# x of two batches brought into the output sum by a TensorE matmul and copied out by ScalarE, and one key-value product moved from GpSimd to VectorE, with all engine queues written in a new order

## What is computed

```
xn = (x - mean) / sqrt(var + eps)
qkv = xn @ w_qkv.T                      # 16 heads of 8
q, k = code products (2 codes per head)
q = softmax(q) * scale
k_exp = exp(k - max over rows of k)
kv = cumsum(k_exp * v) / cumsum(k_exp)  # over the rows of a batch
attn = (q . kv) @ w_out.T
gate, up = fp4(xn) @ fp4(w_gate).T, fp4(xn) @ fp4(w_up).T      # 352 columns
ffn = fp4(silu(gate) * up) @ fp4(w_down).T
out = x + attn + ffn
```

## Time and profile before

| | |
|---|---|
| median of three runs | 129.69 us (129.6 to 129.81) |
| profiled execution, its own time | 129.76 us |
| its span, from first to last instruction | 128.0 us |
| granted TensorE clock, mean | 1.000 |
| TensorE matmul busy | 123.7 us (97%) |
| TensorE weight load busy | 104.7 us (82%) |
| VectorE busy | 119.3 us (93%) |
| ScalarE busy | 103.4 us (81%) |
| GpSimd busy | 116.4 us (91%) |

### The profile page before, as it was taken

The page is one execution under the profiler, slowest core; times in us unless marked ns, Lnnn a source line. Parts: engine busy times, 40 slices in busy tenths (PEclk is TensorE's granted clock), DMA queues, the critical chain, the costliest instruction groups (busy, mean ns, idle before and its releaser), DMA issues.

```text
span 128.0 us, 2411 instructions
## 1 busy us (share of the span) xinstructions
PE 123.7 (97%) x805; PEld 104.7 (82%) x805; DVE 119.3 (93%) x275; ACT 103.4 (81%) x272; POOL 116.4 (91%) x130
## 2 busy tenths in 40 slices
PE   6999999999999999999999999999999999999992
PEld 6988777676666778987678989998877989999991
DVE  3888999999999999999999999999999999999951
ACT  1498989999999998999979489479979976827740
POOL 5499999999999999999999999999999999998800
PEclk9999999999999999999999999999999999999999
DMA  4994000000000000002000020020002000202031
GB/s 101 282 348 176 0 10 3 0 0 0 0 0 0 0 5 0 0 13 74 0 0 3 3 82 5 0 82 0 0 0 82 5 0 0 82 0 87 0 110 54
DMA packets 4363, 5.14 MB, mean 40 GB/s; under 512 B 576, under 2 KB 2432, under 8 KB 4352
## 3 DMA queue, kind: packets, MB, share of 16 engines
q1 hardware_dynamic: 3552, 4.69, 10.6%
q10 hardware_dynamic: 800, 0.31, 0.9%
HBM read 2.90 MB, written 2.10 MB: 39 GB/s over the span
## 4 chain that ended last, share of the span: by engine, by line
PE 79%; ACT 7%; POOL 6%; DVE 3%; DMA 2%; issue 1%; POOLq 0%
PE ps L1905 17%; PE ps L1888 13%; PE ps L1885 11%; PE ps L1892 8%; PE ps L1856 7%; PE ps L1897 5%; PE ps L1875 3%; PE ps L1870 3%; PE ps L1876 3%; DMA x_all<-x 2%; PE ps L1881 2%; PE ps L1865 2%; PE ps L1837 2%; PE ps L1851 2%; POOL yx L374 2%; POOL o_codes L394 2%
## 5 line engine op out<-in xcount | busy, mean ns | idle before, releaser
L1905 PE MATMUL ps<-w_t,hq_t 128*128 128x128 f32 x192 | 25.1, 275 | 0.0
L1905 PEld LDWEIGHTS ps<-w_t,hq_t 128*128 128x128 f32 x192 | 23.7, 192 | 1.6 <-DVE qh L1343 0.3
L399 POOL TENSOR_TENSOR yh<-h,h_r 128x704 f32<-128x704 f32 (+1 forms) x20 | 23.0, 1155 | 0.5 <-ACT h_r L713 0.3
L1888 PE MATMUL ps<-w_t,xq_t 128*128 128x352 f32 x64 | 22.6, 463 | 0.0
L1885 PE MATMUL ps<-w_t,xq_t 128*128 128x352 f32 x64 | 21.6, 463 | 0.0
L404 POOL TENSOR_TENSOR hq<-qh,h_max 128x704 f32<-128x704 bf16 (+1 forms) x16 | 19.9, 1245 | 0.1
L719 ACT ACTIVATE hq_t<-ps 128x384 f32<-128x384 f32 x32 | 15.0, 486 | 5.9 <-PE ps L1892 5.9
L390 POOL TENSOR_TENSOR kv<-kv 128x288 f32<-128x288 f32 x24 | 19.3, 804 | 0.3
L384 POOL TENSOR_TENSOR kv<-v_sb,kv 128x1024 f32<-128x1024 f32 x8 | 15.8, 1977 | 0.3 <-ACT kv L684 0.2
L394 POOL TENSOR_TENSOR o_codes<-kv,q_n 128x1024 f32<-128x1024 f32 (+1 forms) x9 | 16.0, 1779 | 0.0
L1885 PEld LDWEIGHTS ps<-w_t,xq_t 128*128 128x128 f32 x64 | 11.4, 190 | 5.3 <-DVE h L1299 0.5
(11 more groups left out here) (126 smaller groups left out, 297.4 us busy)
## 6 DMA issues: line engine op xcount, KB each, us to landing
x_all<-x SPq DMA_DIRECT2D x8, 256.0 KB, 4.9
out<-out_sb SPq DMA_DIRECT2D x7, 256.0 KB, 2.0
out<-out_sb SPq DMA_DIRECT2D x4, 64.0 KB, 1.6
w_raw<-w_down SPq DMA_DIRECT2D x1, 176.0 KB, 4.6
w_raw<-w_up ACTq DMA_DIRECT2D x1, 128.0 KB, 3.3
w_raw<-w_gate SPq DMA_DIRECT2D x1, 128.0 KB, 3.3
wqk_raw<-w_qkv ACTq DMA_DIRECT2D x1, 128.0 KB, 5.3
wqkv_t<-w_qkv SPq DMA_DIRECT2D x1, 64.0 KB, 4.8
```

The lines of the kernel that those rows point to most:

```text
L399: return nc.gpsimd.tensor_tensor(blocks(yh[:, p, lo * FF:hi * FF], n), h[:, p, lo * HB:hi * HB, 0:BLOCK], spread(h_r[:, p, lo * HB:hi * HB ...
L1888: return nc.tensor.matmul(ps[:, bank, 0:FF], xq_t[:, b % 2, j * P:(j + 1) * P], w_t[:, FFP:FFP + FF], start=True, stop=True)
L1905: last = nc.tensor.matmul(ps[:, bank, j * P:(j + 1) * P], hq_t[:, b % 2, j, c * P:(c + 1) * P], w_t[:, 2 * FFP + c * P:2 * FFP + (c + 1) * P],
```

## The change

Two edits change what is computed where.

1. For batches 0 and 1, `add_x` multiplies the identity with x (one matmul of 512 columns, f32) into the bank in which the output is summed, as the first matmul there. When `project` and `down` have been added, ScalarE's `keep_out` copies the bank to `out_sb`. VectorE's `residual` of these two batches is gone. SyncE's queue waits for `outk_done` instead of `resid_done` for their stores.
2. For batch 0, `k_times_v_from` on VectorE reads v straight from the bank that `qkv` wrote and multiplies it by exp(k), in two instructions of 512 elements. GpSimd's `k_times_v(0)` and ScalarE's `keep_v(0)` are gone.

With them, the queues of all engines are written in a new order. What is new in kind there: `x_dequant` of batch 2 moves from VectorE to GpSimd (and its `x_grid` writes SBUF instead of the bank); `warm_input()` moves on VectorE from ahead of `guards()` to behind `negative_mean(0, 1)`; eight `unread()` stand at the start instead of seven and fifteen in all instead of sixteen; `qk_weights` and its copy come ahead of the first transposes; batch 0's gates all stand behind `w_transpose('up')`, where two of them stood before it. The cut diff:

```diff
+            def keep_out(b, bank):
+                return nc.scalar.activation(out_sb[:, b % 2, :], ps[:, bank, :], ACT.Copy)
...
+            def k_times_v_from(b, bank):
+                p = b % 2
+                for a in range(2):
+                    last = nc.vector.tensor_tensor(kv[:, p, 2 * a:2 * a + 2, 0:KV].rearrange("p j (c h w) -> p j c h w", c=CODE, w=HEAD),
+                                                   halves(bank)[:, a, :, HEADS + HC:].rearrange("p j (h w) -> p j h w", w=HEAD).unsqueeze(2).broadcast_to([P, 2, CODE, HEADS, HEAD]),
+                                                   kv[:, p, 2 * a:2 * a + 2, KV:ROW].rearrange("p j (c h) -> p j c h", c=CODE).unsqueeze(4).broadcast_to([P, 2, CODE, HEADS, HEAD]), ALU.mult)
+                return last
...
+            def add_x(b, bank, start):
+                return nc.tensor.matmul(ps[:, bank, :], ident[:, :], x_all[:, b, :], start=start, stop=False, skip_group_check=True)
```

VectorE's queue at the start:

```diff
-            warm_input().then_inc(warmin_done, 1)
             guards()
             dve.wait_ge(x_in[0], 16)
             statistics(0, 1).then_inc(bn_done, 1)
             statistics(0, 0).then_inc(bn_done, 1)
             dve.wait_ge(bn_done, 2)
             variance(0, 1).then_inc(veps_done, 1)
             negative_mean(0, 1).then_inc(nmean_done, 1)
+            warm_input().then_inc(warmin_done, 1)
```

TensorE's queue (the seven `unread()` ahead of these lines stay):

```diff
-            pe.wait_ge(xn_done, 2)
-            pe.wait_ge(xnp_done, 2)
-            transpose_xn(0, 0).then_inc(xnT_done, 1)
+            unread()
             pe.wait_ge(wqk_in, 16)
             pe.wait_ge(codebd_done, 1)
             qk_weights(1).then_inc(wqk_done, 1)
+            pe.wait_ge(xnp_done, 2)
+            transpose_xn(0, 2).then_inc(xnT_done, 1)
+            unread()
             unread()
             pe.wait_ge(wv_in, 16)
-            pe.wait_ge(wqkev_done, 1)
-            qkv(0, 2).then_inc(qkv_done, 1)
-            unread()
-            unread()
+            pe.wait_ge(xnt_done, 1)
+            qkv(0, 3).then_inc(qkv_done, 1)
             unread()
             unread()
```

More of the change, by code:

```diff
@@ L787, in _ @@
[L787 to L788 removed]
             act.wait_ge(kshift_done, 1)
[L790 to L792 removed]
+            k_exp(0, 3).then_inc(kexp_done, 1)
+            act.wait_ge(gate_T_done, 1)
+            w_keep('gate', 0).then_inc(gate_ev_done, 1)
+            act.wait_ge(xnt_done, 2)
+            act.wait_ge(yx_done, 2)
@@ L1964, in _ @@
-            pe.wait_ge(qx_done, 3)
-            w_transpose('up', 0).then_inc(up_T_done, 1)
-            pe.wait_ge(xq_done, 2)
-            pe.wait_ge(kexp_done, 2)
+            w_transpose('gate', 0).then_inc(gate_T_done, 1)
+            unread()
+            pe.wait_ge(qx_done, 1)
+            pe.wait_ge(gate_ev_done, 1)
+            qkv(1, 0).then_inc(qkv_done, 1)
+            unread()
+            pe.wait_ge(kmax_done, 2)
+            transpose_k_max(1, 0).then_inc(kmaxT_done, 1)
+            pe.wait_ge(xq_done, 1)
@@ new lines, in _ @@
+            pe.wait_ge(xq_done, 2)
+            pe.wait_ge(vsb_done, 1)
+            transpose_xq(0, 2, 4, 0).then_inc(xqT_done, 1)
+            pe.wait_ge(up_dq_done, 1)
+            w_transpose('up', 1).then_inc(up_T_done, 1)
+            pe.wait_ge(xnt_done, 3)
+            add_x(0, 6, True)
+            pe.wait_ge(xqt_done, 1)
+            gate(0, 0, 3).then_inc(gate_done, 1)
+            pe.wait_ge(xqt_done, 2)
+            gate(0, 2, 0).then_inc(gate_done, 1)
+            pe.wait_ge(xnt_done, 4)
@@ new lines, in _ @@
+            add_x(1, 4, True)
+            pe.wait_ge(xq_done, 5)
+            transpose_xq(3, 0, 4, 5).then_inc(xqT_done, 1)
+            pe.wait_ge(wo_in, 16)
+            pe.wait_ge(ot_done, 1)
+            project(0, 6, False).then_inc(wo_done, 1)
+            pe.wait_ge(h2_done, 2)
+            pe.wait_ge(xqt_done, 4)
+            gate(2, 0, 1).then_inc(gate_done, 1)
+            gate(2, 1, 2).then_inc(gate_done, 1)
+            pe.wait_ge(xqt_done, 5)
+            gate(3, 1, 5).then_inc(gate_done, 1)
@@ new lines, in _ @@
+            pe.wait_ge(h2_done, 3)
+            up(3, 0, 2 + 0).then_inc(up_done, 1)
+            up(3, 1, 2 + 1).then_inc(up_done, 1)
+            pe.wait_ge(hq_done, 1)
+            pe.wait_ge(down_q_done, 1)
+            transpose_hq(0, 1, 0).then_inc(hqT_done, 1)
+            pe.wait_ge(silu_done, 15)
+            gate(2, 2, 5).then_inc(gate_done, 1)
+            pe.wait_ge(h2_done, 4)
+            qkv(3, 2).then_inc(qkv_done, 1)
+            pe.wait_ge(hqt_done, 1)
+            transpose_xn(5, 0).then_inc(xnT_done, 1)
@@ new lines, in _ @@
+            down(0, 0, 6, False).then_inc(down_done, 1)
+            pe.wait_ge(hq_done, 4)
+            pe.wait_ge(h2_done, 6)
+            transpose_hq(0, 3, 2).then_inc(hqT_done, 1)
+            transpose_xn(4, 3).then_inc(xnT_done, 1)
+            down(0, 1, 6, False).then_inc(down_done, 1)
+            pe.wait_ge(hqt_done, 4)
+            down(0, 3, 6, False).then_inc(down_done, 1)
+            pe.wait_ge(qh2_done, 1)
+            pe.wait_ge(xnt_done, 6)
+            qkv(4, 0).then_inc(qkv_done, 1)
@@ new lines, in _ @@
+            pe.wait_ge(kneg_done, 6)
+            k_shift(5, 0).then_inc(kshift_done, 1)
+            pe.wait_ge(outk_done, 2)
+            gate(5, 3, 4).then_inc(gate_done, 1)
+            pe.wait_ge(silu_done, 19)
+            gate(4, 1, 2).then_inc(gate_done, 1)
+            pe.wait_ge(silu_done, 20)
+            pe.wait_ge(add3_done, 5)
+            prefix(4, 3).then_inc(base_done, 1)
+            pe.wait_ge(silu_done, 21)
+            pe.wait_ge(xqv_done, 2)
+            up(4, 0, 4 + 0).then_inc(up_done, 1)
```

2206 lines of the change are left out of this document (1073 added, 1133 removed).

## The result

The changed kernel takes 133.02 us (median of four, 132.91 to 134.1), the kernel before beside it 129.75 us (129.6 to 129.89). The ratio is 1.0279, 95% interval 1.0249 to 1.0308: 3.3 to 3.6 us slower. Predicted were 133.5 us, 131.0 to 135.2. The profiled execution took 133.11 us and its span 131.4.

The account below looks back on a forecast made before the run. TensorE's nearly hole-free queue was taken as the bound: mark at 22.85 plus 106.5 us of work puts the last matmul at 129.35, 3.7 us later, so 129.76 + 3.7 = 133.5 us; range 131.0 to 135.2.

Parts of the forecast that it names:

- The late start: Opening fillers on TensorE start at 4.9 us instead of 1.1, and four engines stand still until they are through.
- E: End of the 32 opening matmuls on TensorE: taken as 11.0 us, own range 10.45 to 11.7.
- the mark: End of w_transpose('up') on TensorE, common to both orders: predicted to move from 21.33 to 22.85 us.
- the rival of a fast start: Opening fillers' pace rises early or isn't low; E is 8.5 to 9.5, total 131.0 to 132.0 us; chance 0.15.
- The second edit: Batch 0's product on VectorE takes 1.2 to 1.35 us under x_scale(1), sparing GpSimd 1.97 us ahead of the mark.
- The work behind the mark: TensorE from the mark to the last matmul's end: 104.3 + 1.72 + 1.18 - 0.66 = 106.5 us.
- Edit 1 costs 1.72 us: Two add_x on TensorE, each two instructions of 512 columns at 0.43 us, add 1.72 us behind the mark.
- the check: Without queue reading: last matmul ends at E + 119.2 us, less holes that go away, of which 4.0 us were found.
- Relief of VectorE counted at nothing: VectorE does about 0.7 us less; costed at nothing, as covered by TensorE.
- more holes: Banks held by the sums of x make TensorE wait on gates and ups: 1.6 us, total 135.1; chance 0.14.
- TensorE isn't the bound: GpSimd sets the pace, its 0.9 us less work shows and the late start is absorbed: 127.5 to 129.4 us; chance 0.08.
- A chain of TensorE pieces from there to the end: Predicted sign of being right: from the mark on, the chain of waits consists of TensorE's own work.

Follow-up runs that it names:

- e2: The changed kernel with the first edit undone (no add_x or keep_out, VectorE's residual instead): 134.25 us, ratio 1.0334 to the kernel before.
- e1: The changed kernel with VectorE filling warm_in first again, ahead of guards(): 130.52 us, ratio 1.0064 to the kernel before.
- e6: The changed kernel with the second edit undone (keep_v(0) on ScalarE, k_times_v(0) on GpSimd ahead of x_scale(1)): 135.03 us, ratio 1.0403 to the kernel before.
- e12: The kernel before, in its own order, with the first edit alone (add_x and keep_out for batches 0 and 1): 132.8 us, ratio 1.0238.
- e8: e1 with both add_x left out and keep_out kept, so x is missing from two outputs: 130.55 us, ratio 1.0069 to the kernel before.
- e9: e1 with each add_x issued twice: 131.81 us, ratio 1.0162 to the kernel before.
- e10: e1 with three gates of batch 2, at 36 to 41 us, issued twice: 132.39 us, ratio 1.0205 to the kernel before.
- e11: e1 with the first edit kept for batch 0 only, batch 1 using VectorE's residual again: 130.76 us, ratio 1.0084 to the kernel before.
- e3: The changed kernel with warm_in filled first and the first edit undone: three executions at 131.22 to 131.69 us, ratio 1.012 to the kernel before.
- e7: The changed kernel with three opening unread() fillers instead of eight: median 132.49 us, ratio 1.0224 to the kernel before.
- e5: The kernel before with three gates, at 59 to 67 us, issued twice: 131.54 us, ratio 1.0135.
- e4: The kernel before with only warm_in's filling moved behind negative_mean(0, 1): 132.51 us, ratio 1.0216.

## Why the prediction was right

**The late start.** E, where the opening fillers let `qk_weights` start: 11.0 predicted, 10.57 measured; K, where `keep_qk_weights` starts: 11.45 and 11.14; `qkv(1)` 16.75 and 16.90; the mark 22.85 and 22.65. The queue of ScalarE was the step that mattered, and its idle time of 2.6 us is where it was looked for. The slow stretch came with the first filler, not at a fixed time: the fillers are 0.213 us apart from 4.86 and 0.112 apart from 9.23. So the rival of a fast start is out. That the granted clock reads 1.00 told nothing: the kept traces hold their first clock record at 7.05 us (before) and 9.15 us (after), where the pace rises, and ahead of it there is none. The Trainium skill's rule (TensorE: Matmul & The Clock Gate, part 1), that the array starts throttled and its own activity releases it, is what this trace shows. How near E came is in part luck: the prediction weighed a slow stretch as long as before, 6.0 us, against shorter ones, it lasted 4.4 us here, and with the same opening `qk_weights` starts at 11.27 in e2. What the prediction didn't say is that the late fillers are 2.5 of the 3.3 us (e1). Its own split, 1.5 us for the mark and 2.2 for the work behind it, is an account of TensorE's time and not one of causes. And the earlier trace rows has one of three waits of TensorE in that view; the other two, of 0.3 and 0.2 us, lie ahead of 15.3 us and change nothing behind the mark.

**The second edit.** 1.2 to 1.35 us at K + 5.6 under `x_scale(1)` predicted, 1.21 us at K + 5.57 measured, and the cover is there. Its worth of about 1.8 us (e6) is most of the length of the call that it takes from GpSimd; the prediction had it in the sum without a number of its own.

**The work behind the mark.** 106.5 us predicted, 106.36 measured. The sum hit, and one of its terms doesn't mean what the prediction took it for. "Edit 1 costs 1.72 us" is true in the old order (e12: 0.86 each in the chain) and false in the new one: there the same time comes out without the two `add_x` (e8). Up to 45 us the new order is set by silu and VectorE's `h` as much as by TensorE. TensorE's queue has been filled up to just that limit, so what is added is paid (e9, e10) and what is taken away turns into waiting. With an early start the account of the check closes for e1 as well: 0.9 us less of fillers, 1.72 more of `add_x` and an end 0.7 us later, which leaves the holes as large as before within 0.2 us. That the work fits doesn't say that the work is the cause: with the two `add_x` taken out the holes are 1.7 us larger and the end is the same, so that the sum hit with this term in it is luck as far as the term goes.

**Relief of VectorE counted at nothing.** This is the step that failed. By e8, e11 and e3, undoing it costs about 0.2 us for batch 1 and about 0.5 more for batch 0 in the new order, with each `residual` at the place in time of the copy. There the first edit is a gain of about 0.7 us, not a cost of 1.72.

**The rivals.** Of *more holes* the sign came without the price: silu and `h` end TensorE's waits at 26.8 and 47.8, but the 106.36 us behind the mark are 0.2 us less than the 104.3 of before with the added work of 2.24, so the holes there are no larger. That the held banks cause these waits isn't shown, since no run gives the banks out in another way. Of *TensorE isn't the bound* the part up to 45 us came, while its price didn't: the late start wasn't absorbed there, since ScalarE's and VectorE's work is as late as TensorE's. "A chain of TensorE pieces from there to the end" was wrong until 47.78.

**What stays open.** Which of the moves in the order costs the 0.8 us that e1 still loses: fewer holes were to be had for the 0.8 us of work that it has more, and weren't. Nor is it shown why four of five executions of e7 take longer, or why the slow stretch of the opening fillers isn't of one length.

## What to carry to other kernels

A record without holes says that more work on that engine will be paid, not that less will be rewarded; take the work out (e8) before a gain is credited to removing it, since an order that was tuned to several engines at once has no single bound. A filler that warms an engine has a place in a queue like any call: ask what is queued behind it, and what fills its input. And a copy given to the engine with most idle time still costs when it waits at the head of that engine's queue (e12).

## What the runs showed of the hardware

The slow stretch of TensorE from rest isn't of one length. The same 32 fillers, started at 1.10 us, took 5.53 us (e10), 6.22 (e1) and 6.79 (e3), and started at 4.86 or 4.88, 5.87 (after) and 6.55 (e2). The 28 of the old order took 6.22 us (before), 5.33 (e5) and, started at 4.67, 4.79 (e4). At the fast pace 32 would take 3.6. The granted clock of the profile reads 1.00 all the while, for want of a record: in the twelve traces that hold clock records the first one starts within 0.2 us of the rise in pace, and the traces of e6 and e7 hold none.

With the late start the end of this stretch decides when `qk_weights` starts. Whether it also makes the time vary from one execution to the next isn't shown. The kernels with the late start spread over 0.5 to 1.3 us (after, e2, e4, e6), e5 and e8 to e12 over 0.05 to 0.34 and e1 over 0.7; but the kernel before, which starts early, spread over 1.0 us in ten executions on the chip of e1 to e4.

`v` times exp(k) took VectorE 1.21 us with v read from PSUM, in two instructions of 512 elements, and GpSimd 1.97 us for the 1024 from SBUF.
